# Mamba stage of a decoder: identity loaded alone, pair matrix placed by 32 small transfers, inputs computed half by half, three scan products moved ahead

## The reference

```python
xn = layernorm(x) * ln_w + ln_b
xi, z = jnp.split(xn @ W_in, 2, axis=-1)          # 256 channels each
u = silu(causal_conv(xi, conv_w, 4 taps) + conv_b)
x_dbl = u @ W_xproj                               # dt_r (8), Bm (64), Cm (64)
delta = softplus(dt_r @ W_dt + b_dt)
A = -jnp.exp(A_log)                               # 256 x 64
def step(h, inputs):
    d_t, B_t, C_t, u_t = inputs
    h = h * jnp.exp(d_t[:, :, None] * A) + (d_t * u_t)[:, :, None] * B_t[:, None, :]
    return h, jnp.einsum('bdn,bn->bd', h, C_t)
y = (scan over the tokens + u * D) * silu(z)
out = x + y @ W_out
```

## Time and profile before

| | us |
|---|---|
| median of 3 runs | 1266.48 |
| lowest and highest | 1263.84, 1274.41 |
| span of the profiled execution | 1288.7 |
| PE / DVE / ACT / POOL busy in the span | 1028.3 / 841.0 / 525.7 / 574.0 |

### The profile page before, as it was taken

How to read it: one execution, slowest core, us unless ns; L and a number is a source line. 1 busy time by engine, 2 the same in 40 slices (tenths; PEclk the granted TensorE clock), 3 DMA queues, 4 the chain that set the end, 5 groups by cost and what they waited for, 6 DMA issues and landing times. The chain is left out here.

```text
span 1288.7 us, 30057 instructions
## 1 busy us (share of the span) xinstructions
PE 1028.3 (80%) x12227; PEld 718.2 (56%) x12237; DVE 841.0 (65%) x1508; ACT 525.7 (41%) x1329; POOL 574.0 (45%) x393
## 2 busy tenths in 40 slices
PE   6538877887889999998365798899497999957895
PEld 2127666666774555555265355655377455533795
DVE  5469999999896775567322787487322788855233
ACT  2534444444443742552132274175144577502121
POOL 3389999999964613101435310110524321002232
PEclk9859999999899999999588899899689899978898
DMA  2198899998875000000473000000465000003792
GB/s 114 45 226 213 233 232 230 224 223 228 211 224 190 2 1 1 1 2 1 114 205 110 20 2 1 1 1 2 162 183 192 1 2 2 1 1 95 254 305 83
DMA packets 74376, 139.77 MB, mean 108 GB/s; under 512 B 8144, under 2 KB 28384, under 8 KB 73888
## 3 DMA queue, kind: packets, MB, share of 16 engines
q1 hardware_dynamic: 70272, 129.67, 36.0%
q0 software_dynamic: 3968, 8.18, 1.8%
HBM read 128.06 MB, written 14.82 MB: 111 GB/s over the span
## 5 line engine op out<-in xcount | busy, mean ns | idle before, releaser
L888 ACT ACTIVATE shifted_a<-scores,nmax_a 128x128 f32<-128x128 f32 x768 | 208.6, 389 | 77.4 <-DVE nmax_a L832 75.9
L1445 ACT ACTIVATE decay<-decay 128x1016 f32<-128x1016 f32 x128 | 124.0, 1002 | 152.5 <-PE decay L1331 152.4
L832 DVE TENSOR_REDUCE nmax_a<-scores 128x4 f32<-128x512 f32 x192 | 123.6, 686 | 69.6 <-PE scores L718 67.4
L364 POOL TENSOR_TENSOR rstd<-ve,neghalf 128x4 f32<-128x4 f32 x30 | 31.5, 1051 | 255.9 <-DVE ve L349 255.9
L1331 PE MATMUL decay<-delta,A_pairs 32*128 32x127 f32 x2048 | 83.3, 300 | 75.4 <-DVE small_pack L1489 34.0
L1785 POOL DMA_INDIRECT results<-xs_s x76 | 72.9, 960 | 120.9 <-DVE xs_s L1960 114.5
L838 DVE COPY PTs_a<-PT 128x512 f32<-128x512 f32 x192 | 123.1, 682 | 2.6 <-PE PT L728 2.6
L1331 PEld LDWEIGHTS decay<-delta,A_pairs 32*128 32x128 f32 x2048 | 69.7, 201 | 94.9 <-DVE small_pack L1489 39.4
L728 PE MATMUL PT<-mamba_pack,shifted_a 128*128 128x128 f32 x768 | 106.3, 280 | 4.4 <-DVE PTs_a L838 2.6
L728 PEld LDWEIGHTS PT<-mamba_pack,shifted_a 128*128 128x128 f32 x768 | 82.3, 141 | 30.3 <-issue 19.2
L1303 POOL TENSOR_TENSOR pos_bias<-pos_bias,B 128x1024 f32<-128x1024 f32 x36 | 85.4, 2407 | 1.9 <-DMA pos_bias<-du_rows 1.9
(11 more groups left out here) (482 smaller groups left out, 2272.5 us busy)
## 6 DMA issues: line engine op xcount, KB each, us to landing
pos_bias<-du_rows SPq DMA_DIRECT2D x72, 256.0 KB, 5.2
small_pack<-L3f_w SPq DMA_DIRECT2D x15, 768.0 KB
XN<-du_rows SPq DMA_DIRECT2D x38, 256.0 KB, 5.0
XNT<-du_rows SPq DMA_DIRECT2D x38, 256.0 KB, 5.0
O<-du_rows SPq DMA_DIRECT2D x36, 256.0 KB, 5.0
masked_cos<-du_rows SPq DMA_DIRECT2D x36, 256.0 KB, 5.0
masked_sin<-du_rows SPq DMA_DIRECT2D x36, 256.0 KB, 5.3
small_pack<-L2f_w SPq DMA_DIRECT2D x15, 514.0 KB
```

What stands on the lines that cost most here:

```text
L364: nc.gpsimd.tensor_tensor(rstd[:, bs], ve[:, bs], m.neghalf[:, bs], ALU.pow).then_inc(m.rstd_ready, 1)
L832: nc.vector.tensor_reduce(nmax[:, u % 4, :], scores[u % 4], AX.X, ALU.min).then_inc(m.maxed, 1)
L888: t = nc.scalar.activation(shifted[u % 4][:, j, :], scores[u % 4][:, j, :], ACT.Exp, scale=-1.0, bias=nmax[:, u % 4, j:j + 1])
L1445: nc.scalar.activation(x, x, ACT.Exp).then_inc(decayed, 1)
```

## The change

1. **Identity alone.** The identity's 128 columns of `mamba_pack` are a transfer of their own, ahead of the rest. The cast `identb` waits for X and for it alone. DVE waits for the rest of the pack between the two norms.
2. **Pair matrix by transfers.** POOL's two products are gone, and so is `pair_rows`. In the norm block ACT clears `A_pairs` and `Cz` (4096 columns each) and takes A = exp(A_log); then SP issues 32 transfers from SBUF to SBUF, each of 4 partitions x 2 x 64 numbers. The sign goes into the scan's Exp (`scale=-1.0`). PE waits for all 32 (`pairs_placed`) at the start of the scan block.
3. **Half by half.** PE, ACT and DVE run half 0 through to du before half 1's softplus. Six small functions put the steps in order. ACT ends with a load of the Exp table.
4. **Three products early.** POOL multiplies the first three tiles (`EARLY = 3`) at the end of the inputs block. The ring's order is O, pos_bias (two), masked_cos, masked_sin, XN, XNT, so that only the last two tiles wait for the X sum and for the gates. The store of half 1 opens the scan block.
5. Semaphores of the Mamba stage that are used up serve again in later stages, from the value where they stand (`m.left`).

```diff
             sp.dma_start(m.X[:], d["x"]).then_inc(m.loaded_x, 16)
-            sp.dma_start(m.mamba_pack[:], d["mamba"]).then_inc(m.loaded_mamba, 16)
+            sp.dma_start(m.w("ident"), d["mamba"][:, 0:128]).then_inc(m.loaded_ident, 16)
+            sp.dma_start(m.mamba_pack[:, 128:], d["mamba"][:, 128:]).then_inc(m.loaded_mamba, 16)
...
-            dve.wait_ge(m.loaded_mamba, 16)
+            dve.wait_ge(m.loaded_ident, 16)
             nc.vector.tensor_copy(m.identb[:], m.w("ident"))
...
+            @block.sync
+            def _(sp):
+                sp.wait_ge(zeroed, 1)
+                sp.wait_ge(a_ready, 1)
+                for row in range(32):
+                    q, j, r = row // 8, row // 4 % 2, row % 4
+                    sp.dma_start(A_pairs[row:128:32, :, (4 * q + r) * 2 + j, :], A[row:128:32, :, :]
+                                 ).then_inc(pairs_placed, 16)
+
+            @block.scalar
+            def _(act):
+                zeros = m.neghalf[:, 0:1].to_broadcast([128, IC * 2 * QUADS * STATE])
+                nc.scalar.activation(A_pairs[:].rearrange("p c i n -> p (c i n)"), zeros, ACT.Copy, scale=0.0
+                                     ).then_inc(zeroed, 1)
+                zeros = m.neghalf[:, 0:1].to_broadcast([128, S * 32])
+                nc.scalar.activation(Cz[:].rearrange("p t i -> p (t i)"), zeros, ACT.Copy, scale=0.0)
+                act.wait_ge(m.loaded_mamba, 16)
+                nc.scalar.activation(A[:].rearrange("p c n -> p (c n)"), m.w("A_log"), ACT.Exp).then_inc(a_ready, 1)
...
-            store(0)
-            sp.wait_ge(x_added, 1)
-            sp.wait_ge(g_done, 2 * IC)
+            sp.wait_ge(du_ready, 1)
+            spread.store(sp, du, 0, du_stored[0])
             sp.wait_ge(du_stored[0], 16 * IC)
             for k in range(len(spread.areas)):
+                if k == 5:
+                    sp.wait_ge(x_added, 1)
+                if k == 6:
+                    sp.wait_ge(g_done, 2 * IC)
                 spread.load(sp, k)
-            store(1)
...
+            copy_low(0)
+            add_steps(0)
+            exp(0)
+            copy_b(0)
+            log(0)
+            silu(1)
+            copy_c(0)
+            gate_of(0, 0)
+            copy_low(1)
+            gate_of(0, 1)
+            add_steps(1)
+            copy_b(1)
+            copy_c(1)
+            gate_of(1, 0)
+            gate_of(1, 1)
+            exp(1)
+            log(1)
+            m.load_table(act, ACT.Exp)
...
-            nc.gpsimd.memset(Cz[:], 0.0)
-            pool.wait_ge(a_ready, 1)
             for c in range(IC):
-                nc.gpsimd.tensor_tensor(A_pairs[:, c, :, :, :].rearrange("p i j n -> p (i j) n"),
-                                        bcast_mid(A[:, c, :], 2 * QUADS), bcast_last(m.w("pair_rows"), STATE), ALU.mult)
                 nc.gpsimd.tensor_scalar(D_order[:, c, :], m.w("order"), m.w("Dskip")[:, c:c + 1], None, ALU.mult)
...
+            pool.wait_ge(b_copied, 1)
+            for k in range(EARLY):
+                spread.multiply(nc.gpsimd, k, B2, fed)
...
-                    nc.scalar.activation(x, x, ACT.Exp).then_inc(decayed, 1)
+                    nc.scalar.activation(x, x, ACT.Exp, scale=-1.0).then_inc(decayed, 1)
```

More of the change, by code:

```diff
@@ L1006, in mamba_stage @@
 def mamba_stage(nc, m):
[L1008 to L1012, removed]
     with ExitStack() as outer:
         sb = lambda name, shape, dt=F32: outer.enter_context(nc.sbuf_tensor(name, shape, dt))
+        A, A_pairs = sb("A", [128, IC, STATE]), sb("A_pairs", [128, IC, 2 * QUADS, STATE])
@@ L1042, in place, with store @@
         return k // 16, k // 8 % 2, k % 2, k % 8 // 2
+    def store(self, sp, du, h, stored):
+        batches = slice(h * (B // 2), (h + 1) * (B // 2))
+        for c in range(IC):
+            sp.dma_start(self.rows[batches, c, :, :].rearrange("b r t -> r b t"),
+                         du[:, c, h * HALF:(h + 1) * HALF].rearrange("r (b t) -> r b t", t=S)).then_inc(stored, 16)
     def load(self, sp, k):
@@ new lines, in copy_low, with add_steps, copy_b @@
+            def copy_low(h):
+                act.wait_ge(dt_done, h + 1)
+                nc.scalar.activation(dt_low[:, cols[h]], DTp[:], ACT.Copy).then_inc(dt_copied, 1)
+            def add_steps(h):
+                for c in range(IC):
+                    act.wait_ge(delta_done, h * IC + c + 1)
+                    nc.scalar.activation(delta[:, c, cols[h]], Dp[c][:], ACT.Identity,
+                                         bias=m.w("b_dt")[:, c:c + 1]).then_inc(delta_copied, 1)
+            def copy_b(h):
+                act.wait_ge(b_done, h + 1)
+                nc.scalar.activation(B2[:, cols[h]], Xp[0][:], ACT.Copy).then_inc(b_copied, 1)
@@ L1145, in _, with gate_of @@
+            def gate_of(h, c):
+                act.wait_ge(g_done, h * IC + c + 1)
+                nc.scalar.activation(gate[:, c, cols[h]], Gp[c][:], ACT.Silu).then_inc(g_copied, 1)
             for h in halves:
@@ L1183, in _, with taps @@
             steps = m.dve_steps
-            dve.wait_ge(pads_ready, IC)
-            for h in halves:
+            at = lambda a, h: a[:, :, cols[h]]
+            def taps(h):
                 out = conv[:, cols[h]].rearrange("p (b s) -> p b s", b=HB)
@@ L1199, in _, with softplus @@
                         steps.done(dve, t)
-            at = lambda a, h: a[:, :, cols[h]]
-            for h in halves:
+            def softplus(h):
                 dve.wait_ge(delta_copied, (h + 1) * IC)
@@ L1217, in _ @@
                 nc.vector.tensor_tensor(at(du, h), at(delta, h), at(u, h), ALU.mult).then_inc(du_ready, 1)
+            dve.wait_ge(pads_ready, IC)
+            for h in halves:
+                taps(h)
+            for h in halves:
+                softplus(h)
+        m.left += [(x_done, 2 * IC), (x_copied, 2 * IC), (g_done, 2 * IC), (g_copied, 2 * IC), (conv_done, 2),
+                   (dt_done, 2), (dt_copied, 2), (b_done, 2), (b_copied, 2), (c_done, 2), (c_copied, 2),
+                   (delta_done, 2 * IC), (delta_copied, 2 * IC)]
         @block.gpsimd
@@ L1277, in _ @@
         def _(sp):
+            spread.store(sp, du, 1, du_stored[1])
             for k in range(R, TILES):
```

184 lines of the change are left out of this document (97 added, 87 removed).

## The result

The changed kernel takes 1279.66 us, the median of 4 runs (1274.66 to 1281.83), against 1267.9 for the kernel before (4 runs, 1263.84 to 1274.41) on the same chip. The ratio is 1.0085 with a 95% interval of [1.0053, 1.0116], some 6.7 to 14.7 us more. The forecast was 4.3 us more: the direction is right, the size less than half of what came. The forecast's verdict was "same" within 1%, and at 0.85% that holds, though narrowly: the interval leaves out "no change at all", and 1279.66 itself lies just above the stated range (1256 to 1279) and the line for "slower" (1279.2). Against the 1266.48 from which the prediction counted, the ratio makes 1277.2.

A forecast was written before the change was run, and what follows sets the result against it. The scan was taken as a block of fixed length hung on its start, behind chains. Start -2.5, norm block +12.5, inputs block -5.7, scan and rest 0: +4.3 on 1266.5 gives 1270.8 us, range 1256 to 1279.

The forecast's parts named there:

- Identity alone, -2.5: Start: the cast begins at 4.65 instead of 7.18, the norm block at 5.15, a gain of 2.5 us.
- SP's first issue at 14.4: Norm block: after ACT's table load, two clears (7.5 us) and Exp, SP starts its transfers at 14.4.
- 32 issues at 0.46, 14.7 us: Norm block: SP's 32 transfers issue 0.46 us apart, 14.7 us in all, ends 13.8 and 21.4.
- Rival A: Norm block: tiny transfers cost SP next to nothing, so the time is 1256.4; chance 0.17.
- Barrier behind SP, 0.3: Norm block's end: the barrier waits for SP, through at 29.1, so the inputs block starts at 29.4.
- Half 0 ready 23.7 behind the block's start: Inputs block: du of half 0 comes 23.7 us after the block's start, before at 35.7.
- The cold start of PE, put at 2.0: Inputs block: after idling some 12 us, five PE records cost 0.4 us more each, 2.0 us.
- Half 1 and the exclusion, block 44.1: Inputs block: POOL's early products exclude DVE's last steps, about 3.3 us; the block ends at 44.1 instead of 40.8.
- Scan and rest 0: Scan block and after: fixed length, first scan 3.4 us behind the block's start as before; difference 0.
- Rival B: SP's queue chokes or each issue costs as a load does, 0.67 us: 1278.7 us; chance 0.13.
- Rival D: Inputs block: PE stays at 1.2 GHz throughout, so the first half's gain is absent, +5: 1275.8 us; chance 0.10.
- C: Inputs and scan: half by half pays more, no exclusion and POOL's head start worth 3.3: 1264.2 us; chance 0.15.

The follow-up runs named there:

- Experiment 5: Changed kernel with the 32 transfers issued at the inputs block's head and the loads of rel_pos and mask issued in the norm block: 1254.79 us.
- Experiment 7: Changed kernel with each of the 32 transfers carrying chunk 0 alone, 4 rows of 256 bytes instead of 8: 1276.21 us.
- experiment 8: Changed kernel with 16 of the 32 transfers, PE waiting for 16: 1266.98 us.
- experiment 1: Changed kernel with the 32 transfers issued at the head of the inputs block instead of inside the norm block: 1261.0 us.
- experiment 2: Changed kernel with none of the three early products (EARLY = 0): 1274.41 us.
- experiment 9: Changed kernel with the pair matrix by POOL's two products, the weight pack loaded in one piece and EARLY = 0: 1260.81 us.
- 4: Changed kernel with the pair matrix by POOL's products as before, no transfers, ACT clearing only Cz: 1265.29 us.
- 6: Changed kernel with the 32 transfers at the inputs block's head, rel_pos and mask loads in the norm block, and EARLY = 0: 1255.92 us.

## Why the prediction was right and wrong

It took the right view of the case: the time is set by when the scan can start, the block barrier waits for SP's issues, part 2 costs more than parts 1 and 3 give. Its sum was 6 us too low, nearly all of it in the price of SP's issues, the 32 and the two at the start. By its steps:

- *Identity alone, -2.5: mis-sized, -1.1.* The cast came at 4.43, earlier than the 4.65 forecast. But the step that said "one more issue on SP (0.45) ends before that" failed. SP's last two issues took 1.20 and 1.36 us, where the earlier trace rows have 0.4 for the plain ones, and SP had become the last at the barrier. Why the two got long stays open (see the end). Over the seven kernels with this part and all eight loads in the start, the norm block begins at 5.54 to 6.58, against 7.31 to 7.67 in the three without it. Experiment 5 gets the whole gain: 4.89, 2.8 earlier.
- *SP's first issue at 14.4: 15.28.* Counted from the block's start it is 8.70 us, forecast 9.25; the estimate of 7.5 for ACT's two clears was near (3.62 and 3.60). The block only began later.
- *32 issues at 0.46, 14.7 us: the term that failed most, 18.57 at 0.58.* The range of 0.43 to 0.67 held it. The mistake was in choosing the end near the plain rows, because few rows of data are moved. Experiment 7 shows that the size has little to do with it, and experiment 8 that the price is paid per issue. Rival A, which put the issues at next to nothing, is out. The Trainium skill's page "DMA: Bandwidth & Descriptors" (in the anatomy of a transfer issued by GpSimd, where the fixed cost goes) has about 50 ns for the sequencer's dispatch. By it rival A would have held, and the trace does not agree as far as the engine's time is concerned: SP is held for 0.54 us by an issue of 4 rows of 256 bytes, some ten times that. The prediction carried the figure over to issues of SP, which that part of the page does not treat.
- *Barrier behind SP, 0.3: 0.75.* Together the norm block's end is at 34.60 instead of 29.4: 5.2 late, of which 1.4 is the start, 3.9 the issues, 0.45 the barrier, less 0.55 for ACT.
- *Half 0 ready 23.7 behind the block's start: 23.7.* The cold start of PE, put at 2.0: experiment 1, where PE is awake, has du stored 21.5 behind the block's start (39.10 - 17.56), 2.1 less. The step was right, and mostly for the reason given: the granted clock is 0.59 over the block's first 4 us and 0.50 in experiment 8, the 1.2 GHz level, against 1.00 in experiment 1. The eight records account for 1.6 of the 2.1. The rest comes from a second low stretch that the prediction did not have: PE's four `Xp` records of L1163 at 47.83 take 3.57 us at a granted clock of 0.54 (47.83 to 51.40), where the same four take 1.98 at 1.00 in experiment 1 (L1158 at 29.20). Ahead of it PE worked from the block's start with no gap over 0.7 us, the last 4 us at 1.00; why the clock fell is open.
- *Half 1 and the exclusion, block 44.1: 44.97.* The exclusion was put at 3.3 and is 2.4, the stretch where DVE waits; the 3.1 of experiment 2's whole edit have 0.7 of PE's clock in them. L1294 ends at 75.49, 1.08 us behind the end of POOL's product (74.41), the same 1.08 that the prediction read in the earlier trace rows. The Trainium skill's page "SBUF — State Buffer" (contention on the engine side) describes an exclusive lock of the shared port pair for a whole instruction; the traces agree, here and in experiment 9. So two errors partly cancel. Against the exclusion, 0.9 too long, stands the half before it: DVE's L1292 starts 36.1 behind the block's start, the forecast had the Exp before it end at 34.4, 1.7 too early. In experiment 1 the same step starts 32.9 behind. The 3.2 between the two are the 1.6 of PE's first eight records and the 1.6 of its second low stretch. So the second of these is nearly the whole miss. ACT's waits of 1.23 and 1.12 us before the copies of B and C are not: experiment 1 has them just as long.
- *Scan and rest 0:* the scan block is 2.6 us shorter in this profile, and the table's last column says that nothing is gained or lost behind the first scan. Within that column's spread of 3 us either way the 2.6 are not an effect. No difference of the medians arises behind the scans that this spread would show.

In sum the first scan was forecast 4.3 later and came 10.5 later; the ratio of the times gives 10.8 us (0.0085 of 1268). Rival B (0.67 an issue) came closest to the time, 1278.7, and half of it was true: the issues cost nearly what a load's do, 0.58, just under the 0.6 from which B was to take the forecast's place. Its other half, that PE's whole start would be colder for longer, was not: the price of the cold start does not grow from 7 to 17 us of idleness. Rival D is out as well, since the granted clock is back at 1.00 from 4 us into the block on, but for the one stretch above, and so is C, since the exclusion is there.

What each part is worth, as far as the runs tell: the half-by-half order, with the ring's order and the moved store, moves the first scan by -6.9 (experiment 9), the transfers hidden behind the inputs chain by -3.0 (1 against 4), the identity alone by -1.3 and with the loads moved by -2.6 (means of the norm block's start, with and without), the three early products by +2.2 and +3.5 (experiments 6 and 2). The same transfers in the norm block: +19.1 (change against 1).

## What to carry to other kernels

The 32 transfers cost nothing here where nobody waited for their issue, but each issue is work of the engine that makes it: 0.54 us for 1 KB, 0.58 us for 2 KB. Where blocks end in a barrier of all engines, count the issues of the last queue like instructions, and put a row of small transfers where a long chain of other engines hides it, not into a short block, whatever its data depend on. And where the last stretch ahead of a fixed stage is a chain, the start of that stage is the number to forecast; the rest of the kernel followed it one for one.

## What was not expected of the hardware

- An issue costs SP 0.58 us for 8 rows of 256 bytes and 0.54 for 4: halving what is moved saves 7%.
- SP's seventh and eighth issue in the start took 0.78 to 1.39 us in most of the kernels with the identity alone (0.44 once, in experiment 7), and 0.44 to 0.47 in the kernels without, whose seventh and last is `mask`. In experiment 5 one of the two still took 0.90, after a pause of 1.4 us. Why they are long in the kernels with the identity's transfer was not tried and stays open.
- PE's eight first records took 3.77 us behind a gap of 1.1 us. Behind longer gaps they took 6.10 (6.90), 6.20 (14.10), 5.50 (14.97), 5.36 (15.76), 5.21 (15.89) and 6.24 (17.43): 1.4 to 2.5 us more, with no trend in the length of the gap.
- A low stretch can also come with no gap over 0.7 us ahead of it. With the change PE's four `Xp` records at 47.83 took 3.57 us at a granted clock of 0.54, in experiment 1 the same four took 1.98 at 1.00, and that alone put half 1 back by 1.6 us.
- DVE's L1278, an operation with one tensor as input, is held by POOL's product just as one with two: 3.48 us for 0.69.
